# Relational layers of a graph network on one core: the ring of gathered batches gets eight slots in place of four

## The reference

```python
def _rgcn_layer(x, W, root, bias, src, dst, seg):
    agg = jax.ops.segment_sum(x[src], seg, num_segments=N_REL * N_NODES)
    agg = agg.reshape(N_REL, N_NODES, -1)
    return jnp.einsum('rnd,rde->ne', agg, W) + x @ root + bias
src, dst = (edge_index[0], edge_index[1])
seg = edge_type * N_NODES + dst
h = x
for l in range(N_LAYERS - 1):
    h = jax.nn.relu(_rgcn_layer(h, weights[l], roots[l], biases[l], src, dst, seg))
h = jax.nn.sigmoid(_rgcn_layer(h, weights[-1], roots[-1], biases[-1], src, dst, seg))
```

## Time and profile before

| | us |
|---|---|
| median of 3 runs | 7024.69 |
| lowest and highest run | 7013.26, 7026.60 |
| span of the profiled execution | 7499.8 |
| of it the first relational layer (3523 to 4555) | 1032 |
| the second (4580 to 5625) | 1045 |
| the third (5638 to 6640) | 1002 |

### The profile page before, as it was taken

How to read it: one execution, slowest core, us unless ns; L and a number is a source line. 1 busy time by engine, 2 the same in 40 slices (tenths; PEclk the granted TensorE clock), 3 DMA queues, 4 the chain that set the end, 5 groups by cost and what they waited for, 6 DMA issues and landing times. The chain is left out here.

```text
span 7499.8 us, 87742 instructions
## 1 busy us (share of the span) xinstructions
PE 4435.1 (59%) x18992; PEld 2329.9 (31%) x19133; DVE 4012.2 (53%) x6257; ACT 1792.5 (24%) x2729; POOL 2382.3 (32%) x2285
## 2 busy tenths in 40 slices
PE   4888566217992554788456775556774444430583
PEld 2454465103441222654223332223331122220221
DVE  8986475898996695554222332223331111128895
ACT  1575112006882321443001111001110000010352
POOL 0000000400000353101666665666656666620000
PEclk8999687558995787899777887777886666665896
DMA  1471664326663575145555555555664444443443
GB/s 41 159 235 39 222 245 158 140 92 181 181 180 94 192 262 204 59 156 198 155 163 177 192 192 167 166 160 184 194 185 144 135 137 139 137 129 123 140 134 108
DMA packets 487888, 1181.10 MB, mean 157 GB/s; under 512 B 65242, under 2 KB 272293, under 8 KB 475138
## 3 DMA queue, kind: packets, MB, share of 16 engines
q1 hardware_dynamic: 313518, 570.19, 23.1%
q0 software_dynamic: 140880, 464.72, 20.5%
q10 hardware_dynamic: 33396, 145.09, 5.3%
HBM read 914.86 MB, written 268.11 MB: 158 GB/s over the span
## 5 line engine op out<-in xcount | busy, mean ns | idle before, releaser
L2653 POOL DMA_INDIRECT rel1s_rows<-rel_table,rel1s_at x672 | 652.1, 970 | 408.7 <-issue 345.7
L2653 POOL DMA_INDIRECT rel0s_rows<-rel_table,rel0s_at x672 | 653.7, 973 | 380.4 <-issue 346.6
L2653 POOL DMA_INDIRECT rel2s_rows<-rel_table,rel2s_at x672 | 648.1, 964 | 372.3 <-issue 333.1
L2785 PE MATMUL rel2s_acc<-rel2s_rows,rel2s_hot 128*128 x753 | 393.8, 537 | 469.6 <-issue 412.3
L2126 POOL TENSOR_TENSOR mamb_st<-mam_u,mamb_bc 128x1600 f32<-128x1600 f32 x64 | 230.8, 3606 | 1135.7 <-DMA mamb_bc<-dbc 1135.7
L1677 PE MATMUL gatx_acc<-gatx_w,gatx_feat 128*65 128x400 f32 x1600 | 541.6, 501 | 25.3 <-DVE gatx_w L1569 25.3
L2785 PE MATMUL rel0s_acc<-rel0s_rows,rel0s_hot 128*128 x740 | 332.8, 466 | 302.0 <-issue 212.6
L2785 PE MATMUL rel1s_acc<-rel1s_rows,rel1s_hot 128*128 x702 | 315.9, 464 | 275.9 <-issue 209.2
L1569 DVE SCALAR_TENSOR_TENSOR gatx_w<-gatx_w,gatx_adj 128x1600 f32<-128x1600 f32 x200 | 363.9, 1820 | 0.5 <-ACT gatx_w L1625 0.5
L1416 DVE CUSTOM_DVE_ANT_0 gatm_junk<-gatm_srow,gatm_gone 128x3200 bf16<-128x3200 f32 x100 | 343.5, 3489 | 33.5 <-DMA gatm_srow<-gat_scores 29.1
L1677 PE MATMUL latx_acc<-latx_w,latx_feat 128*65 128x400 f32 x800 | 291.3, 508 | 102.0 <-DVE latx_w L1569 102.0
(11 more groups left out here) (611 smaller groups left out, 9605.8 us busy)
## 6 DMA issues: line engine op xcount, KB each, us to landing
mamb_bc<-dbc SPq DMA_DIRECT2D x128, 800.0 KB, 5.8
agg_strip<-strips SPq DMA_DIRECT2D x100, 800.0 KB, 5.5
gatx_adj<-adj SPq DMA_DIRECT2D x200, 400.0 KB, 3.0
adj<-adj_counts SPq DMA_DIRECT2D x25, 1600.0 KB, 7.1
latx_adj<-adj SPq DMA_DIRECT2D x100, 400.0 KB, 3.0
rel_table<-rel0p_prod POOLq DMA_DIRECT2D x25, 1536.0 KB, 6.2
rel_table<-rel0s_prod ACTq DMA_DIRECT2D x25, 1536.0 KB
rel_table<-rel1s_prod ACTq DMA_DIRECT2D x25, 1536.0 KB
```

The source lines that it names most:

```text
L2653: pool.indirect_dma_start(rows[:, u, k, :], None, table, bass.IndirectOffsetOnAxis(ap=at[:, n:n + 1], axis=0)).then_inc(s_in[u], 16)
L2785: one = nc.tensor.matmul(acc[a][:, :], to, row[:, 0:2 * D], start=fresh and k == 0, stop=False)
```

## The change

It sets the constant SLOTS to 8. That doubles the four buffers of the ring and the semaphores that the gathers count up (`s_in`, one per slot); the pool from which those are taken grows from 36 to 48. PE's and DVE's start values of the counts follow R. The ring takes 4 x 7 KB more in each partition.

```diff
@@ -29,7 +29,7 @@
 RING = 4
 Q = 4
 LEAST = 5
-SLOTS = 4
+SLOTS = 8
 PIECES = 3
@@ -3273,7 +3273,7 @@
         g.waited = ctx.enter_context(nc.semaphore("waited"))
-        g.pool_sems = [ctx.enter_context(nc.semaphore(f"pool_dma{n}")) for n in range(36)]
+        g.pool_sems = [ctx.enter_context(nc.semaphore(f"pool_dma{n}")) for n in range(48)]
```

## The result

| | kernel before | changed kernel |
|---|---|---|
| median of 13 runs each, us | 7026.60 (7013.26 to 7031.04) | 7039.63 (7031.25 to 7047.89) |
| ratio | | 1.0020, interval 1.0013 to 1.0027 |
| span of the profiled execution | 7499.8 | 7040.9 |

The account below looks back on a forecast made before the run. POOL's gathers, 5.0 us per batch, were taken to bound the relational layers in timed runs. From 7024.7 us, slots and memory added 0 and slack took off 4: about 7020 us, own range 7008 to 7036, range given 6900 to 7045.

Parts of the forecast that it names:

- POOL is the floor of a layer at 5.0 us per batch: Relational layers: four gathers of 1.25 us make a batch, so 168 batches take 842 us, whatever the ring does.
- No batch is added, memory and semaphores cost nothing: Ring of eight: 168 batches are 21 x 8, buffers lie in free memory, semaphores are cleared in ranges; 0 us.
- PE's stops come with the recording of the profile: TensorE's stops in the relational layers were taken as absent from timed runs, explaining the profile's 475 us excess.
- My two candidate causes: For PE's stops: trace recording pushing back on engines (gain 0), or code fetched at taken branches (gain 322 us or more).
- The sum, 7024.7 + 0 + 0 - 4: Whole kernel: timed median plus terms for slots, memory and slack, about 7020 us, counted as no change.
- The slack term of minus 4 us: Tile ends: PE may be 7.9 us late, 28 with eight slots; gain 4 us, bounds 0 and 466 us.
- rival C: Relational layers: slower because DVE's row-number copies fall on POOL's gathers; 7079 us if the loss doubles, chance 0.09.
- It decides once the mean grows by 7 ns: Gather's mean time: growth of 7 ns over 2016 gathers, 14 us, is where DVE's interference begins to count.
- rival A: Relational layers: PE's stops are real and the deeper ring absorbs them, gain 322 us, to 6703 us, chance 0.17.
- The sign that I named for C: Gather's mean: a rise above 980 ns, and the time with it, would show DVE slowing POOL's gathers.
- PE's slow pairs will still be there: Changed kernel's profile: slow pairs remain, layers' first-to-last stretch 850 to 950 us, span 250 to 350 us shorter.
- B: Tile ends: part of PE's stops is real, for example 0.8 us at each of 75, to 6965 us, chance 0.13.

Follow-up runs that it names:

- f2: The kernel before (four slots), unchanged, profiled once more in a series without stops: 7029.1 us, one execution.
- e2: Four slots as in the kernel before, only the semaphore pool grown from 36 to 48, with stops: 7513.7 us, ratio 0.9998.
- h1: The changed kernel with row numbers, one-hots and slot release all held at four ahead, without stops: ratio 0.9997 to the kernel before.
- g4: The changed kernel with row numbers, one-hots and slot release all held at four ahead, with stops: 7510.6 us, ratio 0.9996 to the kernel before.
- f1: The changed kernel (eight slots), unchanged, run again beside the kernel before without stops: 7042.9 us, ratio 1.0020.
- e4: The kernel before with eight slots but still 36 semaphores in the pool, with stops: 7792.4 us, ratio 1.0366.
- e1: The kernel before (four slots), unchanged, profiled once more in a series with stops: 7518.3 us, one execution.

## Why the prediction was wrong, point by point

- **POOL is the floor of a layer at 5.0 us per batch: right.** In f2, without stops, 168 batches take 849.5 us in the second layer, and the three layers' gathers take 2542 us where I had 2563.
- **No batch is added, memory and semaphores cost nothing: right.** 672 gathers per layer; e2, h1 and g4 are within 0.04% of before. One detail is off: SyncE's loop is one turn of the ring as well, so its body grows too, not POOL's alone (its register instructions on L2638 go from 126 to 63). h1 has this and costs nothing.
- **"PE's stops come with the recording of the profile": wrong.** They are in whole series of runs and absent from others. For the series that was timed the conclusion held all the same, by luck and not by the reason given: no stops, and POOL hardly ever waits for the ring (2.4 us in f2). My two candidate causes, recording and fetching of code, both predicted something that the runs deny: the first that a recorded run has stops (f2, recorded, took 7029.1 us and has none), the second that every run has them (7026.6 without).
- **The sum, 7024.7 + 0 + 0 - 4: this is the step that failed.** The slack term of minus 4 us is nothing: no ring wait is there to be removed, and POOL's idle time is equal in f2 and f1. And the sum has no term for what VectorE does to the gathers once it may run ahead. That term, rival C's, was left out of it at a chance of 0.09, and it makes nearly the whole of the result, plus 13 to 15 us (18 of the 18.6 us by which f1's gathers are longer).
- **Rival C: right in kind, wrong in instruction and in size.** "It decides once the mean grows by 7 ns" was well placed: the gather's mean went from 958 ns (1931.6 / 2016) to 966 in the changed kernel (1946.5 / 2016) and 967 in f1, and the time by 13 to 15 us, not by 54. I had priced the 504 copies (L2670), which cost nothing; it is the one-hots (L2681), of which 112 more ran at a gather's start. And my argument against it, that POOL hardly stops now either, missed where the new hits come from: not from POOL standing still less, but from VectorE losing the landing that paced it. The prediction itself named the place, in rival A: at a tile's end VectorE waits for PE's sum. I read it as a limit on a gain and not as the start of a burst. The sign that I named for C, a mean above 980 ns, could not have shown it: the changed kernel's 966 is even below the 969 of the profile before (1953.9 / 2016), which has stops; only against f2's 958 does the growth show.
- **"PE's slow pairs will still be there", span 250 to 350 us shorter: wrong.** The changed kernel was profiled without stops, span 458.9 us shorter; had it been profiled with stops, it would have been about 290 us longer than before (e4's 7787.5 against 7499.8).
- **Rival A and B: denied without stops, and reversed with them** (3.7% slower).

## What to carry to other kernels

When a profile's span is far from the timed runs, that profile shows another state of the machine than the time does, and what it shows of waits is to be taken up only if a profile whose span agrees shows it too. A deeper ring is worth something only where a producer really waits for a slot, and it can have a price of its own: an engine that the old depth paced is let loose, and here VectorE's one-hots, which had mostly begun at a harmless point of a gather, fell on its start twice as often. Look at what an engine will be waiting for once the old wait is gone, for an in-order engine the next wait in its program, and at the burst that follows it.

## What the hardware showed unexpectedly

- An indirect DMA of 128 rows takes GpSimd 0.946 us undisturbed. A one-hot of 512 numbers with both inputs in the state buffer, already running at its start, lengthens it by 0.145 us in the mean, and by more where more of the one-hot is still to run; one that begins later inside the gather costs nothing. Four tensor_scalar of 128 numbers in its place lengthen it to as much as 1.549 us, and do so when they begin inside it.
- The same program takes 7026.6 to 7031.0 us in some series of runs and 7509.0 to 7515.5 us in others, on one chip once each. In the latter PE's register instructions on L2785, in the relational layers, take up to 1447 ns (e1) where they take up to 158 ns otherwise (f2), and with eight slots VectorE's on L2681 take up to 1412 ns (e4). The cause is open.
